# A Mamba-2 layer beside a two-expert feed-forward on one core: token statistics in two halves, softplus's series on GpSimd, and a new order of the work around the choice of experts

## What is computed

```python
xn = layernorm(x)                              # over the 128 features
# way 1, a Mamba-2 layer
u = layernorm(xn) * ln_w + ln_b
z, xBC, dt = split(u @ W_in.T)                 # 256 | 512 | 4
dt  = softplus(dt + dt_bias)                   # one step size per token and head
xBC = silu(conv4(xBC) + conv_b)                # four taps along the tokens
A_cs = cumsum(dt * -exp(A_log)) by chunks      # decays; the chunked scan uses exp of their differences
y = scan(xBC, dt, A_cs) + D * xs;  y = rms(y * silu(z)) * rms_w
# way 2, eight experts, two for each token
p = softmax(xn @ router);  w, idx = top_k(p, 2);  w = softmax(w)
moe = sum(w_k * (silu(xn @ gate[idx_k]) * (xn @ up[idx_k])) @ down[idx_k])
out = x + (xn + y @ W_out.T) + moe
```

## Time and profile before

| | us |
|---|---|
| runs (three) | 751.95, 753.68, 761.06 |
| median | 753.68 |
| the profiled execution, as timed | 749.04 |
| its span in the trace | 747.2 |

### The profile page before, as it was taken

How to read it: one execution, slowest core, us unless ns; L and a number is a source line. 1 busy time by engine, 2 the same in 40 slices (tenths; PEclk the granted TensorE clock), 3 DMA queues, 4 the chain that set the end, 5 groups by cost and what they waited for, 6 DMA issues and landing times. The chain is left out here.

```text
span 747.2 us, 15261 instructions
## 1 busy us (share of the span) xinstructions
PE 608.8 (81%) x3702; PEld 516.1 (69%) x3703; DVE 577.9 (77%) x1440; ACT 470.5 (63%) x1014; POOL 425.8 (57%) x622
## 2 busy tenths in 40 slices
PE   0696448888998999999899988769999999999700
PEld 0696226677877777877777777658898888888600
DVE  7676998998988989889889898766666667666354
ACT  0254355788778887788877887446666666666400
POOL 4343006677767667676777657705666666666710
PEclk9999999999999999899999999979999999999955
DMA  9980000000000000000000003333333333332179
GB/s 304 268 174 0 26 6 17 26 26 29 24 26 27 24 23 23 23 26 27 23 23 27 23 24 111 111 89 105 107 113 105 105 105 109 107 106 81 43 289 385
DMA packets 64651, 61.48 MB, mean 82 GB/s; under 512 B 9242, under 2 KB 55710, under 8 KB 64624
## 3 DMA queue, kind: packets, MB, share of 16 engines
q1 hardware_dynamic: 56176, 44.11, 20.6%
q0 software_dynamic: 8448, 17.06, 6.7%
HBM read 30.19 MB, written 31.47 MB: 83 GB/s over the span
## 5 line engine op out<-in xcount | busy, mean ns | idle before, releaser
L479 POOL DMA_INDIRECT moe_d<-raw,slot_st x136 | 133.7, 983 | 91.9 <-issue 69.4
L452 POOL DMA_INDIRECT slots_d<-rows,slot_st x128 | 135.9, 1062 | 74.1 <-POOL rows L447 52.8
L1076 DVE SCALAR_TENSOR_TENSOR act<-raw,taps,act 128x512 f32<-128x512 f32 x192 | 147.6, 776 | 16.6 <-ACT act L541 15.8
L680 ACT ACTIVATE l_sb<-bank 128x256 f32<-128x256 f32 x136 | 44.8, 381 | 73.2 <-PE bank L908 73.2
L428 POOL TENSOR_TENSOR xde<-xb,e_end 128x256 f32<-128x256 f32 x64 | 48.1, 751 | 62.6 <-DVE xb L1149 61.3
L1264 DVE CAST x_hi<-bank 128x256 fp32r<-128x256 f32 x68 | 28.9, 425 | 64.0 <-PE bank L917 64.0
L806 PE MATMUL bank<-xb,m_sb 128*128 128x64 f32 x512 | 71.4, 285 | 6.5 <-POOL xde L428 4.4
L806 PEld LDWEIGHTS bank<-xb,m_sb 128*128 128x128 f32 x512 | 66.7, 200 | 8.3 <-issue 4.6
L936 PE MATMUL bank<-act,raw 128*128 x544 | 71.9, 275 | 0.0
L936 PEld LDWEIGHTS bank<-act,raw 128*128 128x128 f32 x544 | 66.1, 192 | 0.2 <-issue 0.2
L908 PE MATMUL bank<-xw_hi,x_hi 128*128 x136 | 59.9, 440 | 6.0 <-DVE m_sb L1275 6.0
(11 more groups left out here) (233 smaller groups left out, 1692.8 us busy)
## 6 DMA issues: line engine op xcount, KB each, us to landing
slots_d<-rows SPq DMA_DIRECT2D x8, 1122.0 KB, 13.6
rows<-slots_d SPq DMA_DIRECT2D x68, 132.0 KB, 2.2
x_sb<-in_x SPq DMA_DIRECT2D x8, 512.0 KB, 6.4
act<-in_x SPq DMA_DIRECT2D x64, 64.0 KB
xw_hi<-moe_d SPq DMA_DIRECT2D x8, 512.0 KB, 9.1
xw_lo<-moe_d SPq DMA_DIRECT2D x8, 512.0 KB, 9.8
out<-x_sb SPq DMA_DIRECT2D x8, 512.0 KB, 13.3
moe_d<-raw,slot_st POOLq DMA_INDIRECT x136, 2.3
```

The costliest lines, as they stand in the source:

```text
L452: nc.gpsimd.indirect_dma_start(out=slots_d, out_offset=bass.IndirectOffsetOnAxis(ap=slot_st[:, r, c:c + 1], axis=0), in_=rows[:, r, c, :], ...
L479: nc.gpsimd.indirect_dma_start(out=moe_d, out_offset=bass.IndirectOffsetOnAxis(ap=slot_st[:, r, c:c + 1], axis=0), in_=ym[r % R][:, c * D: ...
L680: a = A(l_sb[:, r % 2, c * F:(c + 1) * F], bank[2 + 2 * (r % 2) + c][:, 0:F], ACT.Silu)
L1076: V.scalar_tensor_tensor(out=group_act(par)[:, t, :], in0=proj[:, t, k:k + GT], scalar=taps[:, t, k:k + 1], in1=group_act(par)[:, t, :], o ...
```

## The change

Six things are edited.

1. **Statistics by halves.** `tile_stats`, `variance`, `scale_once` and `scale_twice` work on tiles 0 to 31 first. The loop over tokens starts when these are scaled. The second half's `bn_stats` stand in pieces between (3 and 3 tiles around the first scaling, 4 behind the first two groups, then 6, 6, 6 and 4 in the groups of turns 1 and 2), its variance and scaling in turn 3. On DVE turns 1 to 3 are written out, the others stay a loop; ACT makes the second half's roots in turn 3.
2. **Loads.** Four small loads that routing needs come behind the first half of x with a semaphore of their own, `ld_route`; the other eight stand behind all of x.
3. **Moved to POOL:** the four copies of `ddr0` into `dd_r`, five small tables, and the series of softplus, as 12 `tensor_tensor` and 9 `tensor_scalar` of 128x256, each waiting for the one before. The buffers of the series move from `act` to others, so that the first group can be projected meanwhile. `w_ln` is scaled behind the first two low parts.
4. **PE:** the six bias products (12 passes) go behind the loop into bank 6; the first group's six projections alternate between two banks and no longer wait for the sums; the cumulative sums come behind the projections and the rank matmuls.
5. **DVE:** the choice of experts and the twelve taps follow |dt|, `w_lo` and the reciprocal; the copies and splits of the sums come behind the taps.
6. **ACT:** the first four projections and taps no longer wait for the exponentials of the sums; those follow all six.

```diff
-              for v in [act[:, 768 + i * 256:768 + (i + 1) * 256] for i in range(5)] + [state[:, :]]]
+              for v in [yg[:, 0, :], yg[:, 1, :], sq[:, 0, :], sq[:, 1, :], y_sb[:, 0, :], state[:, :]]]
...
-            for i in range(8):
+            def load_x(i):
                 sp.dma_start(x_sb[:, 8 * i:8 * i + 8, :], x[:, 8 * i:8 * i + 8, :]).then_inc(ld_x[i], 16)
-            for dst, src in ((cols[:, 0:1], ln_w), (cols[:, 1:2], ln_b), (cols[:, 2:6], conv_b), (cols[:, 6:8], d_skip),
-                             (cols[:, 8:10], rms_w), (w_raw, w_in_t), (wdt_sb[:, :], w_dt), (rdt_w[:, 0:E], router),
+
+            for i in range(4):
+                load_x(i)
+            for dst, src in ((cols[:, 0:1], ln_w), (cols[:, 1:2], ln_b), (wdt_sb[:, :], w_dt), (rdt_w[:, 0:E], router)):
+                sp.dma_start(dst, src).then_inc(ld_route, 16)
+            for i in range(4, 8):
+                load_x(i)
+            for dst, src in ((cols[:, 2:6], conv_b), (cols[:, 6:8], d_skip),
+                             (cols[:, 8:10], rms_w), (w_raw, w_in_t),
                              (wo_raw, w_out_t), (dtb_in, dt_bias.broadcast_to([P, NH])),
                              (alog_in, a_log.broadcast_to([P, NH])), (taps[:, :, :], conv_w)):
                 sp.dma_start(dst, src).then_inc(ld_w, 16)
...
+            for i in range(2):
+                for a in range(2):
+                    nc.gpsimd.tensor_copy(dd_r[0:8, i, a * NH * P:(a + 1) * NH * P], ddr0[0:8, :]).then_inc(ddr_done, 1)
...
+            nc.gpsimd.tensor_copy(rev, rev_i).then_inc(tables_done, 1)
+            nc.gpsimd.tensor_copy(iota_f, iota_r).then_inc(tables_done, 1)
+            nc.gpsimd.tensor_copy(meta[:, :, 0, 0], tokid).then_inc(tables_done, 1)
+            chain(nc.gpsimd.tensor_copy(meta[:, :, 1, 0], tokid))
+            nc.gpsimd.tensor_scalar(meta[:, :, 1, 0], meta[:, :, 1, 0], float(NT * P), None, ALU.add)                .then_inc(tables_done, 1)
+
+            pool.wait_ge(ld_route, 16 * 4)
             nc.gpsimd.tensor_tensor(rdt_w[:, E:ROUTE], wdt_sb[:, :], lnw_c.broadcast_to([P, NH]), ALU.mult)\
                 .then_inc(wdt_done, 1)
...
+            pool.wait_ge(ld_w, 16 * 8)
+            nc.gpsimd.tensor_tensor(w_ln, w_raw, lnw_c.broadcast_to([P, DI + CONV]), ALU.mult).then_inc(w_ln_done, 1)
...
+            G = nc.gpsimd
+            pool.wait_ge(recip_done, 1)
+            chain(G.tensor_tensor(th[2], th[2], th[3], ALU.mult))
+            chain(G.tensor_tensor(th[3], th[2], th[2], ALU.mult))
+            chain(G.tensor_scalar(th[1], th[3], 1.0 / 17, 1.0 / 15, ALU.mult, ALU.add))
+            for c in (13, 11, 9, 7, 5, 3, 1):
+                chain(G.tensor_tensor(th[1], th[1], th[3], ALU.mult))
+                chain(G.tensor_scalar(th[1], th[1], 1.0 / c, None, ALU.add))
+            chain(G.tensor_tensor(th[1], th[1], th[2], ALU.mult))
+            chain(G.tensor_scalar(th[1], th[1], 2.0, None, ALU.mult))
+            pool.wait_ge(relu_done, 1)
+            chain(G.tensor_tensor(dts[:, :, :], th[1], th[0], ALU.add))
+            G.tensor_tensor(th[4], dts[:, :, :], a_neg.unsqueeze(1).broadcast_to([P, NT, NH]), ALU.mult)                .then_inc(adt_done, 1)
+
+            pool.wait_ge(norm_done, 4)
...
+            group(NB // 2 - 1, (root_var, root_q))
+            with act_e.Fori(NB // 2, NB) as it:
+                group(it)
...
+            act_e.wait_ge(bias_done, 1)
+            for i in range(NCT):
                 keep_proj(0, i, 0)
-                if i < NCT:
-                    tap0(0, i, 0)
+                if i == 0:
+                    act_e.wait_ge(wdve_done, 1)
+                tap0(0, i, 0)
             act_e.wait_ge(gap_done, 1)
             A(te[3], te[1], ACT.Exp).then_inc(gap_exp, 1)
             act_e.wait_ge(top2_done, 1)
             A(tv[4], tv[3], ACT.Exp).then_inc(top2_exp, 1)
+            act_e.wait_ge(bias_ps, 1)
+            for i in range(NCT, NAT):
+                keep_proj(0, i, 0)
+            act_e.wait_ge(cs_copied, 2)
+            A(e_cs[:, :, :], cs_sb[:, :, :], ACT.Exp).then_inc(e_done, 1)
+            A(e_tot[:, :, :], th[5], ACT.Exp).then_inc(e_done, 1)
+            act_e.wait_ge(dsub_done, 1)
+            A(e_end[:, :, :], th[3], ACT.Exp).then_inc(e_done, 1)
             silu(0, 0)
...
+            pe.wait_ge(ld_w, 16 * 8)
+            for t in range(NAT):
+                c = slice(DI + t * P, DI + (t + 1) * P) if t < NCT else slice((t - NCT) * P, (t - NCT + 1) * P)
+                m = mm(bank[6][:, t:t + 1], w_raw[:, c], lnb_c, start=True, stop=True)
+            m.then_inc(bias_ps, 1)
...
+                elif i > 1:
+                    pe.wait_ge(proj_done, i - 1)
...
             for i in range(NAT):
                 project(0, 0, 0, i)
-
             pe.wait_ge(oh_done, 1)
             ohf = oh_b.rearrange("p t e -> p e t")
             mm(bank[4][:, :], strict_b[:, :], ohf, start=True, stop=True)
             mm(bank[5][:, :], ones_b[:, :], ohf, start=True, stop=True).then_inc(rank_ps, 1)
+
...
+            pe.wait_ge(e_done, 2)
+            pe.wait_ge(csp_done, 4)
+            pe.wait_ge(ddr_done, 4)
+
...
+            tile_stats(0, NT // 2)
+            variance(0, 1)
+            tile_stats(32, 35)
+            scale_once(0)
+            tile_stats(35, 38)
+            scale_twice(0)
 
...
+            tile_stats(38, 42)
...
-            with dve.Fori(1, NB) as it:
+            for it in range(1, NB // 2):
+                for u in range(2):
+                    norm_group(it, u)
+                    if it == NB // 2 - 1 and u == 0:
+                        variance(1, 8)
+                    if it == NB // 2 - 1 and u == 1:
+                        scale_once(1)
+                    routes_kept(it - 1, u)
+                    if it < NB // 2 - 1:
+                        tile_stats(*((42, 48), (48, 54), (54, 60), (60, 64))[it * 2 + u - 2])
+            scale_twice(1)
+            with dve.Fori(NB // 2, NB) as it:
                 for u in range(2):
...
+            dve.wait_ge(w_hi_done, 1)
+            V.tensor_tensor(w_lo[:, :], w_ln, w_hi[:, :].bitcast(F32), ALU.subtract).then_inc(wdve_done, 1)
+            dve.wait_ge(a_exp, 1)
+            chain(V.tensor_scalar(a_neg, a_pos, -1.0, None, ALU.mult))
+            dve.wait_ge(dexp, 1)
+            chain(V.tensor_scalar(th[3], th[2], 2.0, None, ALU.add))
+            V.reciprocal(th[3], th[3]).then_inc(recip_done, 1)
+            dve.wait_ge(bias_ps, 1)
+            V.tensor_copy(proj_b[:, :], bank[6][:, 0:NAT]).then_inc(bias_done, 1)
+            V.tensor_scalar(th[0], th[0], 0.0, None, ALU.max).then_inc(relu_done, 1)
 
```

238 lines of the change are left out of this document (112 added, 126 removed).

## The result

| | before | changed |
|---|---|---|
| median of 20 runs each, side by side, us | 755.49 | 758.51 |
| lowest and highest | 750.51, 761.06 | 752.69, 763.74 |
| ratio of the runs | | 1.0048, interval 1.0025 to 1.0071 |
| the profiled execution, as timed | 749.04 | 755.09 |
| its span | 747.2 | 752.9 |

A forecast was written before the change was run, and what follows sets the result against it. The span before the sequences, set by when DVE has the slots (114.1), was taken as the bound. Loop 7.1 us earlier and part behind it 5.7 longer give -1.4 us: 753.68 becomes 752.3, range 746 to 758.

The forecast's parts named there:

- The measure: Sequences, experts and final sum are untouched, so every microsecond by which their start (114.1) moves is one of the time.
- The start: Ahead of the loop: first matmul at 16.5 us instead of 24.40, a gain of 7.9 us.
- The loop: Loop over tokens: 10.3 us ahead at group 2 become 7.1 at group 9, kept to its end (68.1 becomes 61.0).
- Behind the loop: Loop's end to slots: 8.4 us off DVE, yet 2.5 us longer with stores behind taps, 5.7 with POOL and DVE holds.
- POOL's series: Softplus series behind the loop: 12.7 us without holds, hidden; with holds it ends at 90.6, the taps at 94.9.
- the series on POOL is slow: Rival behind the loop: POOL's steps take 1.27 + 0.07 us, the part is 13.6 us longer, time 760.2; chance 0.10.
- threshold of 1.03 us a step: POOL step time, with `adt_done` at 94.2, from which a slow series eats into the 7.1 us gain.
- signs of being wrong: POOL `tensor_scalar` far over 0.61 us, PE's sums ended after the taps, or first matmuls waiting for something other than DVE.
- The sum: Whole kernel: -7.1 + 5.7 = -1.4 us, so 753.68 becomes 752.3.
- The range of 5 to 9 us for the loop: Lead at loop's end: no DVE loss gives 10.3, another 0.5 us for each of five groups 4.6; 5 to 9 taken.
- the rival of a loop without loss: DVE's groups in turns 1 to 3 stay at 2.54 us: 749.7; chance 0.12, shared with a slower loop (754.4).
- The holds: POOL and DVE partly block each other behind the loop: taps pushed 0.3 us each, ending 3.2 us later; chance 0.40.

The follow-up runs named there:

- exp_early: Changed kernel with the slots' exp on ACT ahead of the first decays instead of behind them and a projection: ratio 1.0028 to the kernel before.
- wln_act: Changed kernel with the scaling of `w_ln` moved from POOL to ACT, as one scaled copy in the loop: ratio 1.0054 to the kernel before.
- all_four: Changed kernel with `w_ln` on ACT, edits of two_op and exp_early, and the sums' copies and splits between sixth and seventh tap: ratio 0.9954 to before.
- head_alone: Changed kernel with series, tables and casts back on DVE and the old order behind the loop; statistics in halves kept: ratio 0.9947 to the kernel before.
- two_op: Changed kernel with a second, value-preserving operation in the eight one-operation `tensor_scalar` of POOL's series: ratio 0.9982 to the kernel before.
- head_wln_act: head_alone with `w_ln` scaled on ACT: median 749.49 us of four runs, ratio 0.9906 to the kernel before.

## Why the prediction was wrong, step by step

- **The measure**, that what moves the start of the sequences moves the time, held in the main. The start moved from 114.77 to 117.52, 2.75 us, inside the 1.9 to 5.4 of the ratio. For eight of the ten kernels with a ratio the shift agrees with the interval too (exp_early lies on its edge). For wln_act (0.4 us later by the start, 4.1 slower by the ratio) and all_four (7.0 earlier, 3.5 faster) it does not; in all_four 1.6 of the difference is the longer first piece.
- **The start:** 16.5 forecast, 17.18 measured. The work between statistics and first normalization was 4.5 us by forecast and 0.1 for POOL's casts and tables; it is 4.05 alone (head_alone) and 1.1 more beside POOL.
- **The loop:** forecast 7.1 us ahead at its end, measured 4.3. This is the step that failed first, and the failed term is a missing one. I wrote that `w_ln` "is now elsewhere" and walked DVE and PE without it, though the diff puts it on POOL behind the first two low parts, beside DVE's normalizations of group 3. Its price is PE's wait of 1.90 us, which is gone in wln_act (the loop ends 2.2 earlier there, 0.4 of it from an earlier first matmul, 16.82). With the start's 0.7 that is 2.6 of the 2.8 missing. The rest of the walk ends nearly right, groups 8 and 9, forecast at 38.9 and 41.5, coming at 39.69 and 42.16 in wln_act, but by two errors of opposite sign (1.0 us less, 1.6 more). Turns 1 and 2 lose nothing to their statistics: they take 5.1 us each, PE's own pace, where the forecast had DVE at 2.9 us a group. Turn 3, with the small operations beside the low parts, takes 8.8 us instead of 7.2; PE's wait of 2.93 us is in it. That part of the walk was luck.
- **Behind the loop:** the path (stores behind the taps, exponents behind the stores, exp behind ACT's other work) was named rightly and its pieces hold: store to exponents 14.5 us (15.7 forecast), exponents to slots 6.0 (6.2), choice and taps pushed from 18.77 to 21.5 us, 2.8 (3.2 forecast). The stores' 1.2 us less took back a third of what the wait for the series cost.
- **POOL's series** is the second failed term: 12.7 us alone by forecast, 17.5 alone in fact. The `tensor_scalar` was taken as 0.43, between a copy and a `tensor_tensor`, with 0.61 as ceiling; the form used takes 0.85, above the ceiling. 0.61 was the row of a `tensor_tensor` with a broadcast input; two full tiles take 0.73. Beside DVE the 18.0 forecast became 23.0. So `adt_done` came 1.4 us behind the taps (91.28 against 89.87), and with PE's sums DVE waited 3.58; two_op gives 2.2 of them back. This is the rival "the series on POOL is slow" in its milder half; its threshold of 1.03 us a step was passed (23.0 / 21 = 1.10), and two of the prediction's own signs of being wrong came true: a `tensor_scalar` far over 0.61 us, and PE's sums ended behind the taps (93.41 against 89.87).
- **The sum:** -4.3 + 7.1 = +2.8 instead of -7.1 + 5.7 = -1.4. Two terms, 2.8 us and 1.4 us off in the same direction, turned the sign. In the prediction's sum either of `w_ln` (1.9) and the one-operation form (2.2) would have been enough to turn it. The range of 5 to 9 us for the loop missed for the same reason: it varied the terms that I had, and held none for one that I had left out. Two small slips are in the prediction's sums: 7.9 and 2.7 us taken from 30.80 give 20.2, not 20.5, for the start of group 2 (measured 21.01), and the rival of a loop without loss, 10.3 us ahead, comes to 749.1, not 749.7. Neither changes its direction.

The holds themselves went as the Trainium skill has it, page "SBUF — State Buffer", section "Who interferes with whom": `tensor_scalar` in a fast mode and operations with two SBUF inputs share a port pair with GpSimd, and the later one "fully blocks". The traces agree for DVE's normalizations behind POOL's long operations (2.98, 3.92, 4.29 us for 1.10), and add that beside back-to-back POOL work at most about one of them got through for each POOL instruction. In the choice and taps DVE lost only 2.8 us over 21, and it was POOL whose steps grew, from 0.85 to 1.17 or 1.35.

## What to carry to other kernels

Work moved to GpSimd is not free for VectorE while both touch SBUF: charge it twice, once at its own price in its exact form (measured, not bounded by neighbours), once as a hold on whatever VectorE does then; ScalarE took the same product in 0.92 us, and no wait of PE grew by it in wln_act. Before work is moved off a busy engine, look for the transfer that the old order hid: here 18 stores and their loads, 14.5 us, mattered more than 8.4 us of VectorE's work. The good half of the change (statistics in halves) was worth 0.5% once the series and the old order were put back (head_alone), and about 0.9% where `w_ln` went to ScalarE as well (head_wln_act, four runs).
